# Window attention in units of eight windows: one pass for the high parts of q and k, one for the low parts, from two neighbouring banks

## The reference

```python
x = x + L0(_gn(x), qkv_w, qkv_b, proj_w, proj_b, rel_table)
x = x + L1(_gn(x))
```

## Time and profile before

| | |
|---|---|
| median of 3 runs | 3903.43 us (3903.14 to 3905.89) |
| the profiled execution's own time | 3903.11 us |
| its span, first to last instruction | 3901.3 us |
| PE busy | 3737.0 us, 96% of the span |
| PE weight loads busy | 3244.5 us, 83% |
| DVE busy | 3169.5 us, 81% |
| ACT busy | 2097.6 us, 54% |
| POOL busy | 1686.3 us, 43% |
| chain of work that ended last | PE 76%, DVE 13%, issue 5%, SP's queue 4% |
| mean granted TensorE clock | 0.992 of full speed |

### The profile page before, as it was taken

One profiled execution on the slowest core, in us unless ns is written; L12 is line 12 of the kernel. 1 busy time (PEld: TensorE's weight loads), 2 busy tenths in 40 slices (PEclk: granted clock), 3 DMA queues, 4 the chain that ended last, 5 costly groups with the idle time before them and its releaser, 6 DMA issues.

```text
span 3901.3 us, 156374 instructions
## 1 busy us (share of the span) xinstructions
PE 3737.0 (96%) x65536; PEld 3244.5 (83%) x65536; DVE 3169.5 (81%) x5647; ACT 2097.6 (54%) x4033; POOL 1686.3 (43%) x1843
## 2 busy tenths in 40 slices
PE   5899999999999999999999999999999999999997
PEld 3788888888888888888888888888888888888887
DVE  5888888888888888888888888888888888888872
ACT  2455555555555555555555555555555555555553
POOL 4544444444444444444444444444444444444430
PEclk9999999999999999999999999999999999999996
DMA  3332232233233233233322322322322332332220
GB/s 81 78 78 68 73 82 69 73 77 74 70 78 77 68 74 79 69 75 77 74 71 74 79 71 73 81 67 73 82 70 71 77 76 69 77 78 58 66 53 20
DMA packets 385728, 280.81 MB, mean 72 GB/s; under 512 B 261927, under 2 KB 384904, under 8 KB 385032
## 3 DMA queue, kind: packets, MB, share of 16 engines
q1 hardware_dynamic: 385032, 270.81, 28.3%
HBM read 39.35 MB, written 38.54 MB: 20 GB/s over the span
## 4 chain that ended last, share of the span: by engine, by line
PE 76%; DVE 13%; issue 5%; SPq 4%; ACT 1%; DMA 1%; POOL 0%; DVEq 0%; ACTq 0%; POOLq 0%
PE pP L460 14%; PE pO L475 11%; PE pS L448 8%; PE pM L558 5%; PE pM L572 4%; PE pM L591 4%; PE pM L584 4%; PE pM L598 4%; PE pM L430 3%; PE pM L381 3%; PE pM L488 3%; PE pM L498 3%; PE pM L388 2%; DVE MX L782 2%; DVE T L775 2%
## 5 line engine op out<-in xcount | busy, mean ns | idle before, releaser
L1058 POOL TENSOR_TENSOR T<-T,MX 128x588 f32<-128x588 f32 x1024 | 1213.0, 1185 | 2114.9 <-DVE MX L782 2114.8
L775 DVE TENSOR_TENSOR T<-pS,table 128x588 f32<-128x588 f32 x1024 | 785.0, 767 | 328.5 <-PE pS L448 313.1
L460 PE MATMUL pP<-K,T 128*128 128x128 f32 x6144 | 870.5, 278 | 0.8 <-issue 0.5
L691 ACT ACTIVATE P<-pP 128x588 f32<-128x588 f32 x1024 | 677.7, 662 | 208.3 <-PE pP L460 202.1
L782 DVE TENSOR_REDUCE MX<-T 128x12 f32<-128x588 f32 x1024 | 768.2, 750 | 2.1
L475 PE MATMUL pO<-V,P 128*49 128x18 f32 x24576 | 716.8, 197 | 39.1 <-DVE O L812 39.0
L475 PEld LDWEIGHTS pO<-V,P 128*49 128x49 f32 x24576 | 696.1, 125 | 46.9 <-ACT P L691 41.4
L460 PEld LDWEIGHTS pP<-K,T 128*128 128x128 f32 x6144 | 674.7, 141 | 26.4 <-issue 0.7
L448 PE MATMUL pS<-KE,QS 128*64 128x196 bf16 (+1 forms) x8192 | 474.1, 234 | 13.0 <-DMA KE<-KS 11.4
L681 ACT ACTIVATE V<-pM 49x384 f32<-49x384 f32 x512 | 264.1, 516 | 376.2 <-PE pM L430 370.0
L448 PEld LDWEIGHTS pS<-KE,QS 128*64 128x64 bf16 x8192 | 290.2, 109 | 180.2 <-issue 94.2
(11 more groups left out here) (95 smaller groups left out, 6787.8 us busy)
## 6 DMA issues: line engine op xcount, KB each, us to landing
KE<-KS SPq DMA_DIRECT2D x512, 147.0 KB, 2.9
KS<-knh SPq DMA_DIRECT2D x768, 49.0 KB, 2.0
QS<-qnh SPq DMA_DIRECT2D x768, 49.0 KB, 2.0
out<-tok_out SPq DMA_DIRECT2D x384, 84.0 KB
tok_in<-x SPq DMA_DIRECT2D x224, 84.0 KB
KS<-knl SPq DMA_DIRECT2D x384, 49.0 KB, 2.0
QS<-qnl SPq DMA_DIRECT2D x384, 49.0 KB, 2.0
tok_in<-x SPq DMA_DIRECT2D x224, 63.0 KB
```

Source lines behind the costliest of these rows:

```text
L460: mm = pe.transpose(pP[:, c, 128 * at:128 * at + 128], T[j % 4][:, 2 * h:2 * h + 2, :], ident)
L691: act.activation(P32[j % 3][:, :, :].rearrange("p (c a) q -> p c a q", c=2), src, ACT.Exp).then_inc(p_made, 1)
L775: dve.tensor_tensor(T[j % 4][:, :, 0:L].rearrange("p (b h) k -> p b h k", b=2), pS[:, :, 0:HALF].rearrange("p b (h k) -> p b h k", k=L), t ...
L1058: pool.tensor_tensor(t, t, MX[j % 4][:, :].unsqueeze(2).broadcast_to([128, HEADS, L]), ALU.subtract).then_inc(shifted, 1)
```

## The change

The tiles `qn` and `kn` become one tile `qkn` per part and buffer with a middle dimension of two. bankB and bankC become the two halves of one tensor of two banks, bankBC; their single names stay as views. `high_qk` is one activation over 2 x 392 columns that waits for k alone. `low_q` and `low_k` become one `low_qk` over 2 x 392 columns, and it stands where `low_k` stood, in slot 2. Four semaphores become two, so whoever waited for a low part of q or of k now waits for both.

```diff
-        qn = [[sb(f"qn{p}{i}", [C, 2 * TOK], BF16) for i in range(2)] for p in "hl"]
-        kn = [[sb(f"kn{p}{i}", [C, 2 * TOK], BF16) for i in range(2)] for p in "hl"]
+        qkn = [[sb(f"qkn{p}{i}", [C, 2, 2 * TOK], BF16) for i in range(2)] for p in "hl"]
...
-        bankA, bankB, bankC = (psum(f"pM{i}", [128, 512]) for i in range(3))
+        bankA = psum("pM0", [128, 512])
+        bankBC = psum("pM12", [128, 2, 512])
+        bankB, bankC = bankBC[:, 0, :], bankBC[:, 1, :]
...
             def stage(S):
...
-                sp.wait_ge(kl_made, 2 * S + 2)
+                sp.wait_ge(qkl_made, 2 * S + 2)
...
-                sp.wait_ge(ql_made, 2 * S + 2)
...
             def wide_squares(G):
...
-                    pe.wait_ge(ql_made, k + QK_AHEAD + 1)
+                    pe.wait_ge(qkl_made, k + QK_AHEAD + 1)
...
             def wide_y(G):
...
-                    pe.wait_ge(kl_made, k + QK_AHEAD + 1)
+                    pe.wait_ge(qkl_made, k + QK_AHEAD + 1)
...
             def high_qk(U):
                 b, s = U // 2 % 2, slice(TOK * (U % 2), TOK * (U % 2) + TOK)
-                act.wait_ge(q_made, U + 1)
+                act.wait_ge(k_made, U + 1)
...
-                act.activation(qn[0][b][:, s], bankB[0:C, 0:TOK], ACT.Copy).then_inc(qh_made, 1)
-                act.wait_ge(k_made, U + 1)
-                act.activation(kn[0][b][:, s], bankC[0:C, 0:TOK], ACT.Copy).then_inc(kh_made, 1)
+                act.activation(qkn[0][b][:, :, s], bankBC[0:C, :, 0:TOK], ACT.Copy).then_inc(qkh_made, 1)
...
-            def low_q(U):
+            def low_qk(U):
                 b, s = U // 2 % 2, slice(TOK * (U % 2), TOK * (U % 2) + TOK)
-                dve.wait_ge(qh_made, U + 1)
-                dve.tensor_tensor(qn[1][b][:, s], bankB[0:C, 0:TOK], qn[0][b][:, s], ALU.subtract
-                                  ).then_inc(ql_made, 1)
-
-            def low_k(U):
-                b, s = U // 2 % 2, slice(TOK * (U % 2), TOK * (U % 2) + TOK)
-                dve.wait_ge(kh_made, U + 1)
-                dve.tensor_tensor(kn[1][b][:, s], bankC[0:C, 0:TOK], kn[0][b][:, s], ALU.subtract
-                                  ).then_inc(kl_made, 1)
+                dve.wait_ge(qkh_made, U + 1)
+                dve.tensor_tensor(qkn[1][b][:, :, s], bankBC[0:C, :, 0:TOK], qkn[0][b][:, :, s], ALU.subtract
+                                  ).then_inc(qkl_made, 1)
...
                 for U in units(s, QK_AT + 1):
-                    low_k(U)
+                    low_qk(U)
...
-                for U in units(s, QK_AT):
-                    low_q(U)
```

More of the change, by code:

```diff
@@ L215, in build @@
         k_made = signal("k_made")
[L216 to L219, removed]
+        qkh_made = signal("qkh_made")
+        qkl_made = signal("qkl_made")
         v_made = signal("v_made")
@@ L307, in stage @@
                     for gq in range(HG):
-                        sp.dma_start(KS[r:128:4, gq, :], kn[part][b][32 * gq:32 * gq + 32, :]
+                        sp.dma_start(KS[r:128:4, gq, :], qkn[part][b][32 * gq:32 * gq + 32, 1, :]
                                      ).then_inc(k_stacked, 16)
-                sp.wait_ge(ql_made, 2 * S + 2)
                 if S >= 2:
@@ L315, in stage @@
                     for gq in range(HG):
-                        sp.dma_start(QS[b][r:128:4, gq, 0:2 * TOK], qn[part][b][32 * gq:32 * gq + 32, :]
+                        sp.dma_start(QS[b][r:128:4, gq, 0:2 * TOK], qkn[part][b][32 * gq:32 * gq + 32, 0, :]
                                      ).then_inc(staged, 16)
@@ L401, in qk @@
                 elif U:
-                    pe.wait_ge(ql_made, U)
+                    pe.wait_ge(qkl_made, U)
                 project(bankB, 0, u, q_made)
@@ L407, in qk @@
                 elif U:
-                    pe.wait_ge(kl_made, U)
+                    pe.wait_ge(qkl_made, U)
                 project(bankC, C, u, k_made)
@@ L496, in project_o @@
                 elif U + 1 + QK_AHEAD < ALL_UNITS:
-                    pe.wait_ge(ql_made, U + 2 + QK_AHEAD)
+                    pe.wait_ge(qkl_made, U + 2 + QK_AHEAD)
                 pe.matmul(bankB[0:C, 0:TOK], PT[:, :], OT[:, :], start=True, stop=True).then_inc(proj_made, 1)
```

## The result

The median after is 3955.31 us (3952.75 to 3955.48, four runs) against 3903.65 us before (3903.14 to 3905.89, four runs): a ratio of 1.0128, interval 1.0114 to 1.0142. The change costs 52 us, or 1.3%. The sum of the prediction had 38 us. The profiled execution took 3955.44 us, 52.3 more than the one before, with a span of 3953.7 us.

The account below looks back on a forecast made before the run. PE was taken as the likely bound, DVE in a few slots. Terms 29.6 + 2.6 + 4.4 - 1.2 + 3.0 = 38.4 us on 3903.11 gave 3941 us; own range 3920 to 3952 (60%), 8 in 10 3905 to 3964.

Parts of the forecast that it names:

- the dearer wait: Rival, 10%: after a real wait PE's next short instructions come late too, another 0.1 us in 211 units; 3962 us.
- The steady unit: Slot 2 of units with a group: `wide_squares` weights at 2.29 us, PE stops 0.17 us; 174 units, 29.6 us.
- instead of 2.12: Slot 2: `wide_squares` weights, formerly 2.12 us behind the scores' start, were to come at 2.29.
- The delay passes on in full: Steady unit: PE's queue behind `wide_squares`, rest of slot 2 and all of slot 3, moves by the whole 0.17 us.
- The first image's nine units: Units before any group: `times_v` 3.92 us behind slot 2's scores instead of 3.59; 9 x 0.33 = 3.0 us.
- the last eight: Units with no load to turn: `wide_squares` 0.77 us later, 0.22 regained at `times_v`; 8 x 0.55 = 4.4 us.
- Without q's pass the chain is done before the scores are, and the bias pass comes at 0.52.: Unit without a group: bias pass 0.46 us earlier, longer pass takes back 0.42; 31 x -0.04 = -1.2 us.
- The one behind the norm chain is counted the same: Unit behind the norm chain in 29 images: priced like a steady unit, 0.17 us each.
- Hidden: Rival, 16%: late weights don't stop the array, as PE may have 0.17 us of issued work left; 3903 to 3907 us.
- Faster: Rival, 6%: merged low pass much cheaper, 0.56 us at two columns a cycle, and DVE's chain sets more; about 3887 us.
- Nothing saved: Rival, 8%: the merged low pass takes 1.11 us, as much as two passes; 73 us more, 3976 us.

Follow-up runs that it names:

- pool_waits: Changed kernel, with GpSimd's `shift` pass ahead of the unit without a group held until the second norm's scale chain ends, once an image; 3942.24 us, ratio 1.0098.
- split_low: Changed kernel with the low pass cut in two again, q then k, both in slot 2 behind the bias pass; 3942.08 us, ratio 1.0098.
- low_only: Changed kernel with the high pass cut in two activations again, so only the low pass is merged; 3952.9 us, ratio 1.0126.
- before_div: Kernel before the change, with the output division ahead of slot 2's maximum; 3918.98 us, ratio 1.0039.
- best_merged: Changed kernel with low pass ahead of bias pass in units with a group, division ahead of maximum, three holds of GpSimd's `shift`; 3878.55 us, ratio 0.9932.
- best_before: Kernel before the change, with the division ahead of the maximum and three holds of GpSimd's `shift` pass; 3867.86 us, ratio 0.9909.

## Why the prediction was right, and where not

**The forecast held in kind**: slower, through a late end of q's low part in slot 2. Its time was 14 us short. The 3955 us lie in the range for 8 in 10 (3905 to 3964), but above the forecast's own (3920 to 3952). They are in the wider one because it made room for the dearer wait, which did not occur; that much is luck.

**The steady unit: mechanism right, size 0.13 for 0.17.** Bias pass at 0.52, low pass at 1.21, end at 2.17 and handoff of 0.11 are the steps as written. The difference is the "instead of 2.12", which was 2.13 in the unit shown, and 0.03 that PE made up at `wide_y`. "The delay passes on in full" was 0.03 too strong. In 174 units the two together made the term 7 us too large.

**The first image's nine units and the last eight**: 0.27 to 0.33 in seven of the nine for 0.33, and 0.74 - 0.20 = 0.54 for 0.55. The 1.8 us that one unit of the first image lost go with its stretch at the lower granted clock: in pool_waits, whose instructions there are the same and whose clock stayed at the upper level, that unit lost 0.32.

**The step that failed: "Without q's pass the chain is done before the scores are, and the bias pass comes at 0.52."** The chain got 0.81 us and was held for 0.74 (0.89 instead of 0.15). The term was -1.2 us and measured 10.8. The pass that was taken away had covered a GpSimd pass. The trace of before had the evidence: line 852, a pass of the same kind, ran from 155 to 1170 ns there, which the same column count can't explain. I had read the mean durations of the large groups alone.

**"The one behind the norm chain is counted the same"**: 0.28 for 0.17. In its timeline after, the bias pass stands 0.57 behind the scores instead of 0.52, since a norm instruction is ahead of it, and `wide_squares` at 2.34. Slot 2 loses 0.19, and 0.09 more go two slots on, where DVE sets the pace. That split was read, not tested.

```profile
1052.03 0.28 PEld L446 LDWEIGHTS pS<-KE,QS 128*64 128x64 bf16 x8
...
1052.60 0.77 DVE L771 TENSOR_TENSOR T<-pS,table 128x588 f32<-128x588 f32 x1 [0.31 <-PE pS L446]
...
1054.37 0.82 PEld L570 LDWEIGHTS pM<-K,SQ 112*96 112x96 f32 x8 [0.18 <-issue]
```

**Left out: the fill.** Ahead of the first scores the next unit's q projection waits for the low part of the unit before, and after the change that means both. I named this waiter and didn't price it. After:

```profile
49.38 0.97 DVE L784 TENSOR_TENSOR qknl<-pM,qknh 96x784 bf16<-96x784 f32 x1 [3.23 <-ACT qknh L668]
...
50.50 0.53 PE L386 MATMUL pM<-XH,WH 97*96 97x392 bf16 x1 [1.26 <-DVE qknl L784]
...
53.55 0.97 DVE L784 TENSOR_TENSOR qknl<-pM,qknh 96x784 bf16<-96x784 f32 x1 [2.73 <-ACT qknh L668]
```

These units follow each other after 4.17 us (53.55 - 49.38). Before, q's low passes began at 50.49 and 53.43, 2.94 apart. Three such intervals are 3.7 us, and 2.9 of them reach the first scores. Either merged pass alone costs as much there: split_low shows 2.4 and low_only 2.2. They have in common that q's low part can't be made before k is projected.

**Open: 2.2 us behind the last scores.** No q or k is made there. What differs is TensorE's granted clock. In the 50 us that end 10 us before the end it was 0.60 before and 0.57 after. The window rows of before_div and split_low for the same 50 us:

```profile
3861.70:3911.70 50.00, 43.16 (x221) 40.76 (x221) 10.68 (x20) 15.25 (x30) 0.00 (x0) 0.50 0.07 18
```

```profile
3881.00:3931.00 50.00, 42.44 (x227) 40.12 (x226) 10.69 (x20) 15.29 (x31) 0.00 (x0) 0.53 0.07 18
```

The stretches behind the last scores are 5.7 us longer than before at 0.50 (before_div, all 50 us at the lower level), 3.5 (best_merged) and 2.0 (split_low) at 0.53, and 0.5 (best_before) to 2.2 (after) at 0.57. So the length goes roughly with the time at that level, in the same work; what sets that time wasn't tested. Differences of a few us between the kernels here can come from it.

**The rivals.** Hidden fell with the steady rows: PE stopped for what was late. Faster fell with a pass of 0.96 us. The dearer wait fell too: behind the late weights 0.03 was made up, nothing more lost. Nothing saved fell with the same 0.96. The time nearest to the measured one, 3962, belongs to a rival that did not occur.

## What to carry to other kernels

Merging two passes makes the first result as late as the second, and it can only start when the later input is there: price the time at which each consumer gets its part, not the engine time saved (39 us of DVE bought a loss of 52). Before a pass is taken off a busy engine, look at what runs on the engines beside it at that moment, since the short instructions behind it may move into something that the pass had covered. Instructions of one kind and size whose longest is several times their shortest are worth a look of their own: here three waits that only keep GpSimd back gained 0.7%, more than half of what the merge lost. And look at the granted clock in each stretch before a miss is put down to an engine: in split_low it went with three quarters of the extra loss in the unit without a group.

## What was not expected of the hardware

Instructions of one column on DVE took as long as a GpSimd pass that was running. The durations of one line in nanoseconds (min/median/max), first in the trace of before, then in that of best_before, where `shift` waits:

```profile
L852 DVE TENSOR_TENSOR g<-mv,g x64: 155/244/1170, 32.2 to 3825.0; 96x1 f32<-96x1 f32 x64
```

```profile
L852 DVE TENSOR_TENSOR g<-mv,g x64: 154/156/156, 32.1 to 3787.7; 96x1 f32<-96x1 f32 x64
```

And the moved instruction in the changed kernel:

```profile
L862 DVE TENSOR_TENSOR g<-g x64: 150/406/925, 42.9 to 3880.1; 96x1 f32<-96x1 f32 x64
```

So a pass of 0.15 us can cost up to 1.17, in the middle of a chain on which the whole unit waits. The hold ends with the GpSimd pass in every place shown (1038.09 and 1038.08; 1044.35 and 1044.33). In the whole trace of the changed kernel, 157 of the chains' instructions with two inputs in SBUF (lines 842, 844, 862, 863, 865 and 866) began inside a GpSimd pass, and 155 of them ended 0.01 to 0.02 us behind it; the 227 others took 0.22 us at most. Large passes with one input in PSUM don't feel it at all: q's low pass before took 0.56 us both in the 70 units where a GpSimd pass ran beside it and in the 186 where none did. The merged low pass never had one beside it in the changed kernel; in pool_waits it had in 31 units, and took 0.96 us there too.
